# One vector step moved four turns later and one small matmul moved one step later, in a fused decoder kernel on one core

## The chip, the cores and the metric

The kernel runs on one core of one Trainium2 chip. The metric is device time in microseconds (us) of one execution; lower is better. A core has a matrix engine (PE, with its own queue PEld for loading the stationary operand), a vector engine (DVE), an activation engine (ACT), a general engine (POOL) and a queue engine (SP) that here only issues DMA transfers. Each engine works through its own instruction list in order, and they meet at semaphores.

## The reference, cut to what matters

Two sequences of 512 tokens with 1024 channels pass through a layer of three parts: a state-space mixer followed by a gated feed-forward block ("stage one" below), a product with a fake-quantised context, and a second gated feed-forward block whose weights are formed from two tensors ("stage two").

```
h   = res + mamba2(rmsnorm(x, ln1_w), ...)          # eight blocks of 128 channels per sequence
h2  = rmsnorm(h, ln2_w)                             # needs the sum of squares over all channels
mlp = silu(h2 @ gate_w.T) * (h2 @ up_w.T) @ down_w.T        # INTER = 3584
...
q1, q2 = fake_quant(x), fake_quant(ctx);  x = x + q1 @ q2
...
d = w - base                                        # w1/mean_w1, w3/mean_w3, w2/mean_w2
W = base + mean(abs(d)) * sign(d)
x = x + (silu(x @ W1.T) * (x @ W3.T)) @ W2.T
```

## The kernel before, in words

Every fp32 product is made of three fp32r products: each operand is split into a rounded high part (ACT copies it, `hi`) and the rest (DVE subtracts, `lo`), and PE does hi by hi, lo by hi and hi by lo. A **step** of PE is 12 matmuls of 128x128 by 128x512: four blocks of the contraction times these three.

Both feed-forward stages (m = 0 and m = 1) have the same plan. `feed_forward(first, last)` on PE walks numbered steps w. The gate and up weights come in 14 pairs of 256 rows. Pair 0 takes 16 plain steps (`plain`, L1011, steps 0 to 15, counted from the start of the stage); each later pair takes 14 steps of a seven-product scheme (`product`, L1067), so pair 1 has steps 16 to 29 and pair 2 begins with step 30. The down projection follows (`down_step`, L1092). Split weights stand in a ring of seven slots: step w reads slot w % 7, which ACT fills (`ring_hi`, L1323) and DVE completes (`ring_lo`, L1779). PE's step w waits for `ring_lo` of w.

On ACT and DVE, `feed_forward(m)` is a loop over turns i that runs ahead of PE. In turn i DVE makes, where tables say so, a combination of the activations or its low parts (`make`, `part_lo_of`), takes the result of step i - 1 out of PSUM (`gate_up_out`), forms a sum of weights for step i + 6 (`weight_sum`), writes `ring_lo` of step i + 5 (`weight_lo`), and then does one extra job that a table gives to the turn. In stage one the extra job is `coeff_diff` (L1923), a difference of two weight tiles that ACT turns into signs and a sum of absolute values (L1449, L1452). In stage two it is `form_weight` (L1947): one instruction on 128x1024 elements,

```
STT(form_tile(f), sign_in[f % 4], coef[:, kind:kind + 1], form_tile(f), ALU.mult, ALU.add).then_inc(s_form, 1)
```

which turns the raw tile (`raw_odd` for odd pairs, `raw_even` for even ones) into the weights of stage two in place. It waits for the raw tile and for the signs, both brought by SP's DMAs. `FORM_AT` gives the turn of every forming, numbered f. Numbers 0 to 3 are pair 0 and are done before the loop; 4 to 7 are the four tiles of pair 1. Four sign tiles exist, and SP loads the signs of f + 4 one turn after the forming of f. Before the loop begins SP issues the two `raw_odd` loads and the signs of 4 to 7; the first of them waits until all four activation quarters of stage two are made, because they are read from where `raw_odd` is written.

ACT's turn is similar: high parts of activations, `weight_hi` of step i + 5, in stage one the signs and absolute values of the turn before, then copies and SiLU of PE's results. The last SiLU of a pair (L1401) must be done before PE starts the next pair, since both use one PSUM bank.

In front of stage one the mixer's output projection gives sixteen blocks of 128 channels, eight per half (one half is one sequence). DVE adds their squares up (`rms_add`, L2223), and PE sums over partitions with one matmul against ones, `rms_sums(h)` (L983; the trace shows it as two passes). ACT and DVE make the scale of the half from it and then the quarters b12 and b22 of the activations. Quarters b11 and b21 belong to the first half and are made earlier; steps 0 to 7 use only these, so that PE has work while the second half is normalised.

Of the kernel before, what the change touches and what calls it, by code (L numbers as in the profile page):

```python
# [61 lines left out]
BASE_G = (0, NG + ND)  # L62
# [5 lines left out]
def turn_no(p, turn):  # L68
    return turn if p == 0 else NP + 14 * (p - 1) + turn
# [19 lines left out]
def step_of(w):  # L89

    m = 0 if w < W_END[0] else 1
    if w < BASE_G[m] + NP:
        return m, "f", 0, (w - BASE_G[m]) // 2, (w - BASE_G[m]) % 2
    if w < BASE_D[m]:
        p, i = divmod(w - BASE_G[m] - NP, 14)
        return m, "g", p + 1, i // 2, i % 2
    d, k = divmod(w - BASE_D[m], SC_PAIRS)
    return m, "d", d // 7, d % 7, k
# [37 lines left out]
def _form(p, turn, what):  # L136
    FORM_AT[turn_no(p, turn)] = len(FORM_NO)
    FORM_NO[what] = len(FORM_NO)
# [3 lines left out]
for _p in range(PAIRS):  # L142
    if _p == PAIRS - 1:
        for _t in (0, 3, 6, 9):
            _form(_p, _t, ("d", next(_down)))
        continue
    _first = _p == 0
    _form(_p, 3 if _first else 0, ("g", _p + 1, 0, 0))
    if not _first:
        _form(_p, 2, ("d", next(_down)))  # L150
    _form(_p, 5 if _first else 4, ("g", _p + 1, 0, 1))
    _form(_p, 7 if _first else 6, ("g", _p + 1, 1, 0))
    _form(_p, 9 if _first else 8, ("g", _p + 1, 1, 1))
    if not _first:
        _form(_p, 10, ("d", next(_down)))
assert next(_down, None) is None
# [31 lines left out]
def build(nc, x_t, ctx, w_mamba, w_dt, w_gu, w_dn, f_gu, f_dn, b_gu, b_dn, params, shapes_only,  # L188
# [637 lines left out]
    def _(pe):  # L826
# [154 lines left out]
        def rms_sums(h):  # L981
            pe.wait_ge(s_sqd, (KT - 1) * (h + 1))
            pe.matmul(bank(6 + h), ones[:, :], rms_sum[:, h, :], start=True, stop=True).then_inc(s_rv, 1)  # L983
# [15 lines left out]
        def plain(w, m, j, x):  # L999

            pe.wait_ge(s_wlo, w + 1)
            name, quad = PLAIN[j][1:]
            out = bank(PLAIN_BANK[quad][x])
            slot = w % RING
            for kk in range(KH):
                if j in (0, 1, 4, 5) and x == 0:
                    pe.wait_ge(s_tlo, n_lo(m, name, kk))
                col = slice(kk * P, (kk + 1) * P)
                hi, lo = part_hi(m, name)[:, kk, :], part_lo(m, name)[:, kk, :]
                for n, (wt, a) in enumerate(((WRH, hi), (WRH, lo), (WRL, hi))):  # L1010
                    ins = pe.matmul(out, wt[:, slot, col], a, start=j % 2 == 0 and kk == 0 and n == 0,  # L1011
                                    stop=j % 2 == 1 and kk == KH - 1 and n == 2, skip_group_check=True)
            ins.then_inc(s_pd, 1)
# [57 lines left out]
        def down_step(w, m, sc, t, k):  # L1071

            pe.wait_ge(s_wlo, w + 1)
            u = w - BASE_D[m]
            pe.wait_ge(s_ulo, m * ND + u + 1)
            d = sc * 7 + t
            if k == 0:
                if d >= 2:
                    pe.wait_ge(s_do, 4 * (m * 14 + d - 1))
                elif d == 0:  # L1080
                    pe.wait_ge(s_c12, 2 * (PAIRS - 1) * (m + 1))
                else:
                    pe.wait_ge(s_gs, 4 * PAIRS * (m + 1))
                    pe.wait_ge(s_pr[2], PAIRS * (m + 1))
                    if m == 0:
                        pe.wait_ge(s_ab, CF_BLOCKS)
            slot, us = w % RING, u % RING
            for q in range(KH):
                out = bank(4 * (d % 2) + q)
                col = slice(q * P, (q + 1) * P)  # L1090
                for n, (wt, a) in enumerate(((WRH, ur_hi(us)), (WRH, ur_lo(us)), (WRL, ur_hi(us)))):
                    ins = pe.matmul(out, wt[:, slot, col], a, start=t in (0, 1, 3) and k == 0 and n == 0,  # L1092
                                    stop=k == SC_PAIRS - 1 and n == 2, skip_group_check=True)
            ins.then_inc(s_pd, 1)

        def feed_forward(first, last):
            for w in range(first, last):
                m, stage, i, j, l = step_of(w)
                if stage == "f":
                    plain(w, m, j, l)  # L1100
                elif stage == "g":
                    product(w, m, i, j, l)
                else:
                    down_step(w, m, i, j, l)
# [43 lines left out]
                ins = pe.matmul(out, row_weights, mean_rows(b, part).bitcast(F32), start=part == 0, stop=part == 1)  # L1148
            ins.then_inc(s_csumd, 1)

        feed_forward(BASE_G[0], BASE_G[0] + 1)
        rms_sums(1)
        feed_forward(BASE_G[0] + 1, BASE_G[0] + 2)
        pe.wait_ge(s_h, BATCH * KT)
        feed_forward(BASE_G[0] + 2, W_END[0] - 4)
        pe.wait_ge(s_xs, 1)
# [81 lines left out]
    def _(act):  # L1238
# [86 lines left out]
        def inner_hi(w):  # L1325

            m, _, sc, t, k = step_of(w)
            u = w - BASE_D[m]
            gen = 64 * (2 * m + sc + 1)
# [73 lines left out]
        def plain_gate(w):  # L1403

            m, _, _, j, x = step_of(w)
            if j % 2 == 0 or x == 1:
                return
            if j == 1:
                if m == 0:
                    act.wait_ge(s_xsum, 16 * BATCH * KT)  # L1410
                else:
                    act.wait_ge(s_x2, 32 * KT)
                act.wait_ge(s_tv, B22_MADE[m])
            quad = PLAIN[j][2]
            act.wait_ge(s_pd, w + 1)
            act.activation(G[m][:, quad, :], bank(PLAIN_BANK[quad][0]), ACT.Silu).then_inc(s_gs, 1)

        def psum_copy(w):

            m, _, p, t, x = step_of(w)  # L1420
            pp = m * PAIRS + p
            done = 2 * n_before(pp)
            if t == 0:
                if p > 1 and x == 0:
                    act.wait_ge(s_c22, done - 2 + 1)
                elif p > 1:
                    act.wait_ge(s_pr[3], pp)
                act.wait_ge(s_pd, w + 1)
                act.activation(TX[m][:, x, :], bank(BANK_B[x]), ACT.Copy).then_inc(s_x1, 1)
            elif t == 2:  # L1430
                if p > 1 and x == 0:
                    act.wait_ge(s_c12, done - 2 + 1)
                elif p > 1:
                    act.wait_ge(s_pr[1], pp)
                act.wait_ge(s_pd, w + 1)
                act.activation(TU[m][:, x, :], bank(BANK_B[x]), ACT.Copy).then_inc(s_u2, 1)
            elif t == 3:
                if x == 0:
                    act.wait_ge(s_c11, done + 1)
                else:  # L1440
                    act.wait_ge(s_pr[0], pp + 1)
                act.wait_ge(s_pd, w + 1)
                act.activation(TX[m][:, x, :], bank(BANK_C[x]), ACT.Copy).then_inc(s_c5, 1)
# [994 lines left out]
```

## Time and profile before

| quantity | value |
|---|---|
| median of 3 runs | 2155.32 us (2153.18 to 2155.93) |
| the profiled execution, its own time | 2155.74 us |
| its span, first to last instruction | 2153.9 us |
| PE busy | 2105.2 us (98% of the span) |
| DVE busy | 1664.3 us (77%) |
| ACT busy | 1070.0 us (50%) |
| mean granted clock of PE | 0.991 of full speed |

Busy shares are means over the whole program. PE's 98% says that nearly all time is matmuls; what is left to gain or lose is in the few places where PE stands still, and in the matmuls behind a pause that run at a lower clock. A start time printed for a matmul is the one to reckon with: in an undisturbed stream a matmul is shown as 0.39 us long, but the next starts 0.23 us after it.

### The profile page before, as it was taken

The numbers are of one execution on the slowest core, as the hardware profiler recorded it, in microseconds if no ns is written. First come the engines' busy times: TensorE is split into PE (matmuls) and PEld (weight loads), VectorE is DVE, ScalarE is ACT, GpSimd is POOL, SyncE is SP. The second block draws the span as 40 slices with busy tenths as digits, with TensorE's granted clock in tenths as the row PEclk, the third lists the DMA queues.
The fourth block names the chain that finished last, engine by engine and source line by source line (L and its number), as shares of the span: only waits on it lengthen the run. The fifth ranks groups of instructions, "written<-read, shape, count | busy, mean of one in ns | idle before, by whom it ended". The sixth has DMA issues, their size and how long they took to land.

```text
span 2153.9 us, 26614 instructions
## 1 busy us (share of the span) xinstructions
PE 2105.2 (98%) x9266; PEld 1684.2 (78%) x9270; DVE 1664.3 (77%) x2497; ACT 1070.0 (50%) x1764; POOL 182.1 (8%) x296
## 2 busy tenths in 40 slices
PE   7999999999999999999999999899999999999999
PEld 3777778778888878888888854788888888888887
DVE  7776666698777878887979898887777677788885
ACT  4333344457777777774444466443333333444442
POOL 0000110101111111210000002001000000100000
PEclk9999999999999999999999999999999999999999
DMA  3151115638989999888250044554444444756101
GB/s 123 40 186 50 57 59 175 171 75 287 311 294 309 344 320 328 307 308 337 90 184 1 1 166 105 152 186 152 159 171 147 164 147 147 287 194 197 63 20 59
DMA packets 136434, 370.06 MB, mean 172 GB/s; under 512 B 16688, under 2 KB 27568, under 8 KB 132656
## 3 DMA queue, kind: packets, MB, share of 16 engines
q1 hardware_dynamic: 111216, 288.16, 39.1%
q0 software_dynamic: 25088, 80.23, 11.0%
q8 instruction: 73, 1.20, 0.2%
q14 instruction: 57, 0.47, 0.1%
HBM read 288.12 MB, written 84.41 MB: 173 GB/s over the span
## 4 chain that ended last, share of the span: by engine, by line
PE 82%; DVE 10%; ACT 4%; issue 2%; DMA 2%; SPq 0%; DVEq 0%; ACTq 0%
PE pair L1067 41%; PE pair L1092 24%; PE pair L839 6%; PE pair L832 2%; PE pair L1011 2%; DVE conv_out L2099 1%; DMA ctx_in<-ctx 1%; DVE ring_lo L1779 1%; PE pair L949 1%; DVE pair L1923 1%; PE pair L970 1%; PE pair L848 1%; DVE weights_lo L1689 1%; PE pair L1125 1%; PE pair L972 0%
## 5 line engine op out<-in xcount | busy, mean ns | idle before, releaser
L1067 PE MATMUL pair<-comb_hi,ring_hi 128*128 128x512 f32 x1456 | 567.3, 390 | 3.3 <-ACT gate_a L1401 3.3
L1067 PE MATMUL pair<-comb_hi,ring_lo 128*128 128x512 f32 x1456 | 567.2, 390 | 0.0
L1067 PE MATMUL pair<-comb_lo,ring_hi 128*128 128x512 f32 x1456 | 567.1, 389 | 0.0
L1092 PE MATMUL pair<-inner_ring_a,ring_hi 128*128 128x512 f32 x1120 | 344.8, 389 | 0.0
L1067 PEld LDWEIGHTS pair<-comb_hi,ring_hi 128*128 128x128 f32 x1456 | 273.7, 188 | 61.7 <-DVE ring_lo L1779 4.9
L1067 PEld LDWEIGHTS pair<-comb_hi,ring_lo 128*128 128x128 f32 x1456 | 273.7, 188 | 57.0
L1067 PEld LDWEIGHTS pair<-comb_lo,ring_hi 128*128 128x128 f32 x1456 | 273.7, 188 | 56.6
L1092 PEld LDWEIGHTS pair<-inner_ring_a,ring_hi 128*128 128x128 f32 x1120 | 210.2, 188 | 43.5
L1092 PE MATMUL pair<-inner_ring_a,ring_lo 128*128 128x512 f32 x560 | 217.9, 389 | 0.0
L1323 ACT ACTIVATE ring_hi<-ring_sum 128x512 fp32r<-128x512 f32 x160 | 101.0, 632 | 142.0 <-DVE ring_sum L1764 140.3
L1092 PE MATMUL pair<-inner_ring_b,ring_hi 128*128 128x512 f32 x448 | 138.3, 390 | 0.0
L1779 DVE TENSOR_TENSOR ring_lo<-raw_a,ring_hi 128x512 fp32r<-128x512 f32 x146 | 99.4, 685 | 50.1 <-ACT ring_hi L1323 50.1
L1449 ACT ACTIVATE sign_out<-pair 128x1024 int8<-128x1024 f32 x84 | 85.9, 1023 | 80.7 <-DVE pair L1923 80.7
L1092 PEld LDWEIGHTS pair<-inner_ring_a,ring_lo 128*128 128x128 f32 x560 | 105.1, 188 | 21.9
L839 PE MATMUL pair<-act_hi,weights_hi 128*128 128x512 f32 x256 | 109.3, 427 | 1.6 <-DVE act_lo L2168 1.4
L1779 DVE TENSOR_TENSOR ring_lo<-ring_sum,ring_hi 128x512 fp32r<-128x512 f32 x160 | 109.5, 684 | 1.5 <-ACT ring_hi L1323 0.2
L1923 DVE TENSOR_TENSOR pair<-coeff_in 128x1024 f32<-128x1024 f32 x84 | 103.0, 1226 | 0.8 <-DMA coeff_in<-b_gu 0.8
L1689 DVE TENSOR_TENSOR weights_lo<-weights_raw,weights_hi 128x1024 fp32r<-128x1024 f32 x44 | 54.6, 1240 | 59.5 <-ACT weights_hi L1246 31.1
L839 PE MATMUL pair<-act_hi,weights_lo 128*128 128x512 f32 x256 | 100.3, 392 | 0.0
L839 PE MATMUL pair<-act_lo,weights_hi 128*128 128x512 f32 x256 | 100.1, 391 | 0.0
L1092 PEld LDWEIGHTS pair<-inner_ring_b,ring_hi 128*128 128x128 f32 x448 | 84.1, 188 | 17.8 <-issue 0.5
L1323 ACT ACTIVATE ring_hi<-raw_a 128x512 fp32r<-128x512 f32 x146 | 90.3, 625 | 8.4 <-PE pair L1011 5.6
(374 smaller groups left out, 3586.1 us busy)
## 6 DMA issues: line engine op xcount, KB each, us to landing
coeff_in<-f_gu SPq DMA_DIRECT2D x56, 512.0 KB, 5.2
coeff_in<-b_gu SPq DMA_DIRECT2D x56, 512.0 KB, 6.8
weights_raw<-w_mamba SPq DMA_DIRECT2D x44, 512.0 KB, 3.4
raw_a<-w_gu SPq DMA_DIRECT2D x28, 512.0 KB, 7.3
raw_a<-w_gu SPq DMA_DIRECT2D x56, 256.0 KB, 6.3
u_spill<-gate_a POOLq DMA_DIRECT2D x56, 256.0 KB, 5.8
coeff_in<-f_dn SPq DMA_DIRECT2D x28, 512.0 KB, 4.4
coeff_in<-b_dn SPq DMA_DIRECT2D x28, 512.0 KB, 6.6
```

Of the source, the lines that this page charges most:

```text
L832: ins = pe.matmul(out[:, HALF[half]], w[:, wi, k * P:(k + 1) * P], a(half, k), start=k == 0 and n == 0, stop=k == KT - 1 and n == 2)
L839: ins = pe.matmul(out, w[:, wi, k * P:(k + 1) * P], a(b, k), start=k == 0 and n == 0, stop=k == KT - 1 and n == 2, skip_group_check=True)
L848: return pe.matmul(out[:, HALF[b]], ones[:, :], src[:, HALF[b]], start=first, stop=last)
L949: pe.matmul(ps[2][:, g * 512:(g + 1) * 512], bx_cur[:, 2 + g, :], xbc[:, 4 + g * HPG:4 + (g + 1) * HPG, b * SEQ + c * P:b * SEQ + (c + 1) ...
L1011: ins = pe.matmul(out, wt[:, slot, col], a, start=j % 2 == 0 and kk == 0 and n == 0, stop=j % 2 == 1 and kk == KH - 1 and n == 2, skip_gro ...
L1067: ins = pe.matmul(out, wt[:, slot, col], a, start=t in (0, 1, 3) and kk == 0 and n == 0, stop=kk == KH - 1 and n == 2, skip_group_check=True)
L1092: ins = pe.matmul(out, wt[:, slot, col], a, start=t in (0, 1, 3) and k == 0 and n == 0, stop=k == SC_PAIRS - 1 and n == 2, skip_group_chec ...
L1323: act.activation(WRH[:, slot, :], src, ACT.Copy).then_inc(s_whi, 1)
L1449: act.activation(sign_out[:, c % 2, :], dif_ps[:, :], ACT.Sign).then_inc(s_sign, 1)
L1689: TT(WL[:, slot, :], raw[:, rslot, :], WH[:, slot, :].bitcast(F32), ALU.subtract).then_inc(s_ready, 1)
L1779: TT(WRL[:, slot, :], src, WRH[:, slot, :].bitcast(F32), ALU.subtract).then_inc(s_wlo, 1)
L1923: TT(dif_ps[:, :], dif[:, c % 2, 0, :], dif[:, c % 2, 1, :], ALU.subtract).then_inc(s_cd, 1)
```

## The change

Two things are moved, nothing is added or removed. In stage two the four formings of pair 1 stand at turns 7, 8, 9 and 10 in place of 3, 5, 7 and 9. The table serves SP too, so its loads of the signs 8 to 11 move along. On PE the matmul `rms_sums` of the second half stands behind step 1 of stage one in place of behind step 0.

```diff
     _first = _p == 0
-    _form(_p, 3 if _first else 0, ("g", _p + 1, 0, 0))
+    _form(_p, 7 if _first else 0, ("g", _p + 1, 0, 0))
     if not _first:
         _form(_p, 2, ("d", next(_down)))
...
-    _form(_p, 9 if _first else 8, ("g", _p + 1, 1, 1))
+    _form(_p, 10 if _first else 8, ("g", _p + 1, 1, 1))
...
-        feed_forward(BASE_G[0], BASE_G[0] + 1)
+        feed_forward(BASE_G[0], BASE_G[0] + 2)
         rms_sums(1)
-        feed_forward(BASE_G[0] + 1, BASE_G[0] + 2)
         pe.wait_ge(s_h, BATCH * KT)
         feed_forward(BASE_G[0] + 2, W_END[0] - 4)
```

DVE's list in stage two before, from `ring_lo` of step 8 to `ring_lo` of step 12 (`comb_...` are combinations of activations, `gate_b` is a result taken out, `raw_odd<-sign_in...` a forming):

```order
L1779 TENSOR_TENSOR ring_lo<-raw_even,ring_hi 128x512
L1947 SCALAR_TENSOR_TENSOR raw_odd<-sign_in_ab,coeff,raw_odd 128x1024
L1862 TENSOR_TENSOR gate_b<-pair,gate_b 128x512
L1779 TENSOR_TENSOR ring_lo<-raw_even,ring_hi 128x512
L1831 TENSOR_TENSOR comb_lo_f_14_128<-comb_lo_f_15_129,comb_lo_f_14_128 128x512 x4
L1779 TENSOR_TENSOR ring_lo<-raw_even,ring_hi 128x512
L1947 SCALAR_TENSOR_TENSOR raw_odd<-sign_in_ab,coeff,raw_odd 128x1024
L1851 TENSOR_TENSOR comb_lo_115<-comb_lo_f_15_129,comb_hi_85 128x512 x4
L1779 TENSOR_TENSOR ring_lo<-raw_even,ring_hi 128x512
L1834 TENSOR_TENSOR comb_hi_f_16_102<-comb_lo_f_14_128,comb_hi_f_16_102 128x512 x4
L1779 TENSOR_TENSOR ring_lo<-raw_even,ring_hi 128x512
```

The same stretch now, on to the first forming (the line numbers are one lower, since the file has one line less):

```order
L1778 TENSOR_TENSOR ring_lo<-raw_even,ring_hi 128x512
L1861 TENSOR_TENSOR gate_b<-pair,gate_b 128x512
L1778 TENSOR_TENSOR ring_lo<-raw_even,ring_hi 128x512
L1830 TENSOR_TENSOR comb_lo_f_14_128<-comb_lo_f_15_129,comb_lo_f_14_128 128x512 x4
L1778 TENSOR_TENSOR ring_lo<-raw_even,ring_hi 128x512
L1850 TENSOR_TENSOR comb_lo_115<-comb_lo_f_15_129,comb_hi_85 128x512 x4
L1778 TENSOR_TENSOR ring_lo<-raw_even,ring_hi 128x512
L1833 TENSOR_TENSOR comb_hi_f_16_102<-comb_lo_f_14_128,comb_hi_f_16_102 128x512 x4
L1778 TENSOR_TENSOR ring_lo<-raw_even,ring_hi 128x512
L1946 SCALAR_TENSOR_TENSOR raw_odd<-sign_in_ab,coeff,raw_odd 128x1024
```

The first forming stood between `ring_lo` of steps 8 and 9; it now stands behind `ring_lo` of step 12, and the other three behind those of 13, 14 and 15. All four were ahead of `ring_lo` of step 15 before; now three are.

PE's list around `rms_sums` before, at the end of step 0 (`comb_hi_75`, `comb_lo_103` are the first half's activations):

```order
L1011 MATMUL pair<-comb_lo_103,ring_hi 128x512
L1011 MATMUL pair<-comb_hi_75,ring_lo 128x512
L983 MATMUL pair<-rms_sum,ones 128x512
L1011 MATMUL pair<-comb_hi_75,ring_hi 128x512
L1011 MATMUL pair<-comb_lo_103,ring_hi 128x512
```

In the changed list twelve more matmuls of step 1 stand ahead of the L983 row, and behind it the first one of step 2:

```order
L1011 MATMUL pair<-comb_lo_103,ring_hi 128x512
L1011 MATMUL pair<-comb_hi_75,ring_lo 128x512
L983 MATMUL pair<-rms_sum,ones 128x512
L1011 MATMUL pair<-comb_hi_76,ring_hi 128x512
L1011 MATMUL pair<-comb_lo_104,ring_hi 128x512
```

SP's list changes in one place: the signs of 8 to 11 were loaded ahead of both loads of pair 2's raw tile (`raw_even`). The load of the signs of 11 now stands between these two, and its wait for the fourth forming holds back the second of them.


## Rows read from the trace of the kernel before

**Rows 1.** The page: the span.

```profile
span 2153.9 us, 26614 instructions
```

**Rows 2.** Waits of PE, whole span: total us, times, longest us.

```profile
PE pair L1011 <- DVE ring_lo L1779: 7.0, 2, 6.4
...
PE pair L1067 <- ACT gate_a L1401: 3.3, 4, 1.9
...
PE pair L983 <- DVE rms_sum L2223: 2.6, 1, 2.6
```

**Rows 3.** PE in time, stage one: start, length, line, tiles, [idle before <-releaser].

```profile
440.62 0.39 PE L1011 MATMUL pair<-comb_hi,ring_lo 128*128 128x512 f32 x1
443.59 1.12 PE L983 MATMUL pair<-rms_sum,ones 128*128 128x512 f32 x2 [2.57 <-DVE rms_sum L2223]
...
448.20 0.39 PE L1011 MATMUL pair<-comb_hi,ring_hi 128*128 128x512 f32 x1
```

**Rows 4.** PE in time, the same sum of the first half.

```profile
402.88 0.40 PE L839 MATMUL pair<-act_hi,weights_lo 128*128 128x512 f32 x1
...
404.21 0.40 PE L839 MATMUL pair<-act_lo,weights_hi 128*128 128x512 f32 x1
```

**Rows 5.** DVE in time, stage one.

```profile
479.21 1.29 DVE L1779 TENSOR_TENSOR ring_lo<-raw_a,ring_hi 128x512 fp32r<-128x512 f32 x2
...
511.74 0.69 DVE L1881 TENSOR_TENSOR gate_a<-first_copy_a,pair 128x512 f32<-128x512 f32 x1 [2.44 <-PE pair L1067]
512.34 0.68 DVE L1779 TENSOR_TENSOR ring_lo<-raw_a,ring_hi 128x512 fp32r<-128x512 f32 x1
...
514.43 0.69 DVE L1881 TENSOR_TENSOR first_copy_a<-first_copy_a,pair 128x512 f32<-128x512 f32 x1 [0.26 <-PE pair L1067]
...
517.17 0.69 DVE L1891 TENSOR_TENSOR gate_a<-second_copy_a,pair 128x512 f32<-128x512 f32 x1
```

**Rows 6.** ACT in time, stage one.

```profile
511.28 0.63 ACT L1323 ACTIVATE ring_hi<-raw_a 128x512 fp32r<-128x512 f32 x1
...
522.85 0.60 ACT L1401 ACTIVATE gate_a<-pair 128x512 f32<-128x512 f32 x1
```

**Rows 7.** PE in time, first matmul of the third pair of stage one.

```profile
525.04 0.39 PE L1067 MATMUL pair<-comb_hi,ring_hi 128*128 128x512 f32 x1
```

**Rows 8.** PE in time, stage two.

```profile
1357.32 0.39 PE L1011 MATMUL pair<-comb_hi,ring_lo 128*128 128x512 f32 x1
1364.14 0.80 PE L1011 MATMUL pair<-comb_hi,ring_hi 128*128 128x512 f32 x1 [6.43 <-DVE ring_lo L1779]
...
1383.98 0.50 PE L1011 MATMUL pair<-comb_hi,ring_hi 128*128 128x512 f32 x1 [0.60 <-DVE ring_lo L1779]
...
1386.63 0.39 PE L1011 MATMUL pair<-comb_hi,ring_lo 128*128 128x512 f32 x1
```

**Rows 9.** DVE in time, stage two.

```profile
1351.95 0.68 DVE L1779 TENSOR_TENSOR ring_lo<-raw_even,ring_hi 128x512 fp32r<-128x512 f32 x1
1361.60 1.28 DVE L1947 SCALAR_TENSOR_TENSOR raw_odd<-sign_in_ab,coeff,raw_odd 128x1024 f32<-128x1024 int8 x1 [8.97 <-DMA sign_in_ab<-sign_spill]
...
1383.25 0.68 DVE L1779 TENSOR_TENSOR ring_lo<-raw_even,ring_hi 128x512 fp32r<-128x512 f32 x1
```

**Rows 10.** Chain of waits, stage two: start, length, what.

```profile
1350.81 10.69 DMA sign_in_ab<-sign_spill
```

**Rows 11.** ACT in time, stage two.

```profile
1422.90 0.58 ACT L1401 ACTIVATE gate_b<-pair 128x512 f32<-128x512 f32 x1
```

**Rows 12.** PE in time after two other pauses.

```profile
396.86 0.50 PE L839 MATMUL pair<-act_hi,weights_hi 128*128 128x512 f32 x1 [1.42 <-DVE act_lo L2168]
...
795.25 0.47 PE L1067 MATMUL pair<-comb_hi,ring_hi 128*128 128x512 f32 x1 [1.94 <-ACT gate_a L1401]
```

**Rows 13.** Two stretches: us, PE busy (instructions), granted clock, DMA share, GB/s.

```profile
795.20:799.60 4.40, 4.35 (x13) 0.63 0.88 292
1364.10:1369.40 5.30, 5.26 (x12) 0.50 0.19 69
```

More of the change, by code:

```diff
@@ L147 @@
     _first = _p == 0
-    _form(_p, 3 if _first else 0, ("g", _p + 1, 0, 0))
+    _form(_p, 7 if _first else 0, ("g", _p + 1, 0, 0))
     if not _first:
         _form(_p, 2, ("d", next(_down)))
-    _form(_p, 5 if _first else 4, ("g", _p + 1, 0, 1))
-    _form(_p, 7 if _first else 6, ("g", _p + 1, 1, 0))
-    _form(_p, 9 if _first else 8, ("g", _p + 1, 1, 1))
+    _form(_p, 8 if _first else 4, ("g", _p + 1, 0, 1))
+    _form(_p, 9 if _first else 6, ("g", _p + 1, 1, 0))
+    _form(_p, 10 if _first else 8, ("g", _p + 1, 1, 1))
     if not _first:
```

## The prediction, made before the result was known

> **What bounds the kernel now.** I read the page first: the whole program is 2153.9 us long [rows 1] and PE is busy nearly throughout, so time can only be won or lost where PE stands still or runs slowly. The waits of PE say where: `ring_lo` holds it up twice for 7.0 us in all, 6.4 of them at once, the second half's `rms_sum` once for 2.6 us, and the SiLU L1401 four times for 3.3 us [rows 2]. The first two are what the change touches. Then I went to the engines in order of time around both.
>
> An undisturbed PE starts a matmul every 0.2267 us: from the tenth matmul of step 1 at 448.20 [rows 3] to the first of step 30 at 525.04 [rows 7] there are 3 + 28 x 12 = 339 starts in 76.84 us. A step is 2.72 us.
>
> **Stage two.** After `ring_lo` of step 8 (started at 1351.95, done at 1352.63) DVE stands for 8.97 us before the first forming, which waits for its signs [rows 9]. The chain of waits shows these signs issued at 1350.81 and landed 10.69 us later, at 1361.50 [rows 10]. `ring_lo` of step 9 is queued behind the forming, so PE, through with step 8, stands for 6.43 us until 1364.14 [rows 8]. What follows runs at half clock: 0.50 granted from 1364.10 to 1369.40, the 1.2 GHz level [rows 13]. At step 15 it waits again, 0.60 us [rows 8]. Sum: from the last matmul of step 8 (1357.32) to the last of step 15 (1386.63) PE took 29.31 us for 7 x 12 = 84 starts, which undisturbed are 19.04 us. So 10.27 us are to be had.
>
> Can DVE now deliver? An instruction of 0.68 us is followed 0.60 us after its start (511.74 and 512.34 in [rows 5]), so it can go on at 1352.55 instead of 1361.60. From there to the start of `ring_lo` of step 15 at 1383.25 [rows 9] it worked without a pause for 21.65 us; one of the four formings (1.28 long, 1.20 net) no longer stands ahead. 1352.55 + 21.65 - 1.20 = 1373.0, done at 1373.68. Undisturbed, PE reaches step 15 at 1357.55 + 6 x 2.72 = 1373.87. That is 0.2 us to spare, the tightest of these steps. The steps before have more: no forming stands ahead of `ring_lo` 9 to 12, and one more comes with each of 13, 14 and 15.
>
> The forming itself moves to turn 7, behind `ring_lo` of 12. The list shows 17 operations of 512 columns from 1352.55 to there: 17 x 0.60 = 10.2, so it starts at about 1362.8, which is 1.3 us behind the landing at 1361.50 [rows 10]. So its wait is hidden by work that DVE has anyway. All four formings end at about 1373.0 + 0.6 + 1.2 = 1374.8, 1.8 us before PE wants step 16 at 1376.6, and `ring_lo` of 16 is directly behind.
>
> Later on DVE is 9.05 us earlier than before and PE 10.27, so DVE's lead over PE is 1.2 us thinner. Step 16 had 2.3 us (`ring_lo` done at 1383.25 + 0.60 + 0.68 = 1384.53 against 1386.86), and the order of work behind it gives the later ones more. The last place where it counts is the SiLU L1401 before step 30: started at 1422.90, done at 1423.48 [rows 11], now at 1414.43. PE began step 30 at 1386.63 + 0.23 + 14 x 2.72 = 1424.94, now at 1414.67. Again 0.2 us to spare. Value taken: 10.3 us. Bounds: the least is 7, if both margins fail by a microsecond and one pause takes PE's clock down; the most is 10.3, since the stalls hold no more.
>
> SP's loads: the second load of pair 2's raw tile is now held until the fourth forming, about 1 us later against PE than before. DVE needs it only at turn 22, about 19 us after, against some ten for the slowest transfer here [rows 10]. Nothing.
>
> **Stage one.** PE ends step 0, waits 2.57 us for `rms_sum` and starts `rms_sums` at 443.59; behind it the clock is down [rows 3]. From the last matmul of step 0 (440.62) to the tenth of step 1 (448.20) are 7.58 us for ten starts, 2.27 undisturbed. The matmul itself costs, at full clock in the first half, 4.21 - 2.88 = 1.33 us for two starts that would take 0.45: 0.87 us [rows 4]. So the pause with its slow tail costs 7.58 - 2.27 - 0.87 = 4.44 us. With step 1 in front PE arrives at 440.85 + 2.72 = 443.57, when the sum is just ready; `rms_sums` runs at the same moment as before, and nothing on ACT and DVE behind it moves. PE is 4.4 us ahead at step 2.
>
> That lead meets DVE and ACT, which stay where they were. `ring_lo` of step 15 ends at 479.85 [rows 5]; PE now wants it at 444.46 + 13 x 2.72 = 479.82, a tie. In pair 1 DVE and ACT hand each other coefficient differences, signs and absolute values, and only their waits for PE can shrink: 2.44 us before L1881 at 511.74, of which 0.4 count, because the `ring_lo` behind it (512.34) then waits for the `ring_hi` of 511.28 + 0.63 [rows 5, 6]; then 0.26 at 514.43 with some 0.1 of rounding, and 0.2 between there and 517.17, where 2.5 us of work take 2.74 [rows 5]. In all 0.95 us. So L1401, done at 523.45 [rows 6], is done at 522.5. PE wants step 30 at 525.04 - 4.44 + 0.1 = 520.7 and waits some 1.7 us. Of 4.4 us there remain 525.04 - 522.5 - 0.1 = 2.4. From there DVE waits for PE again and keeps in step. Bounds: at least 0.8, if the clock falls behind this new pause (next paragraph); at most 4.4, if L1401 follows PE fully.
>
> Does the clock fall? After a pause of 1.42 us the next matmul was 0.50 long and no slow ones followed; after one of 1.94 us [rows 12] the granted clock was 0.63 over the next 4.4 us: 13 matmuls where 19.4 fit, some 1.5 us lost [rows 13]. The new pause of 1.5 to 1.7 us lies between. I take the milder, as the nearer; the other is a rival. TensorE: Matmul & The Clock Gate, section "What's actually happening", in the Trainium skill, says that the number of slow matmuls at a start differs from run to run of one kernel. No run here shows that yet; by it every slow tail above, those removed too, could be one or two microseconds longer or shorter.
>
> **Sum.** 10.3 + 2.4 = 12.7 us. The profiled execution took 2155.74 us, 1.84 more than its span; less 12.7 that is 2143.0. It stands 0.42 above the median of the runs, so the median should be 2155.32 - 12.7 = 2142.6 us.
>
> **Rivals.**
> - A, the forecast: 2142.6, own range 2141.4 to 2143.8. Chance 0.45.
> - B, stage one keeps all its 4.4 us, because ACT catches up in pair 1. For it: L1401 did not hold PE at this step before [rows 5 to 7]. Against it: the count above. 10.3 + 4.4 = 14.7, so 2140.6. Chance 0.12.
> - C, the new pause before step 30 takes the clock down: 12.7 - 1.5 = 11.2, so 2144.1. Chance 0.18.
> - D, the signs come late. DVE now takes out its result at 1352.55 and POOL stores it (256 KB) while the signs are on their way; before, that store began after 1363. If the signs landed 4 us later, at 1365.5, the first forming would wait 2.75 us and step 15 start 2.55 late, with a slow tail of 1.5: 12.7 - 4.05 = 8.65, so 2146.7. It decides from 1.5 us of lateness on. Chance 0.14. DMA: Bandwidth & Descriptors, section "Issuing engines are not separate DMA queues", in the Trainium skill, says that transfers of SP and POOL run on the same 16 engines and interleave, which speaks for it; the trace shows 10.69 us for one sign tile among them.
> - E, the L1401 region from 690 to 840 us, where it waits already, swallows stage one's gain, as its pace comes from DMA: 10.3, so 2145.0. Chance 0.06.
> - F, the other side: PE, arriving early, pauses before each of the 13 pairs of stage one and each pause costs the slow tail of 1.5 us. 13 x 1.5 = 19.5 against 12.7: slower by 6.8, so 2162.1; it decides from nine pairs on. Against it: a PE that lost 1.5 us is later at the next pair and waits less, and the waits there were four [rows 2]. Chance 0.03.
> - G, the change doesn't do what it says: the first forming finds its raw tile missing, a megabyte issued just before the signs, and stands as long as now. Then only stage one's 2.4 us remain: 2152.9. Against it: at 1361.60 the tile was there. Chance 0.02.
>
> What a measurement can tell from no change is 0.2%, 4.3 us. A to E are faster by more: 0.95; I give 0.94. G is within: 0.03, F slower: 0.03. The range reaches from just under B to just over D: 2140.0 to 2147.0.
>
> **What would show each step.** Right: DVE shows no wait for `sign_in_ab` at the first forming, PE's wait for `ring_lo` is gone or under 0.5 us, and the stretch behind step 8 has full clock; L983 has no wait, and step 2 of stage one starts at about 444.5; PE shows one new wait of 1.5 to 1.7 us for L1401 near 520.7. Wrong: a wait of DVE for signs or for `raw_odd` near 1360 (D, G); half clock behind 522 (C); no wait there (B); L1401 waits in sum over 3.3 + 1.7 us (E, F).

## The result, and the profile after

The changed kernel takes 2142.75 us (median of 5 runs, 2141.25 to 2146.65); the kernel before took 2154.68 us beside it (5 runs, 2153.18 to 2155.93). The ratio is 0.9948, 95% interval 0.9938 to 0.9959, so the change is worth 11.2 us, between 8.8 and 13.4. The forecast was 2142.6. Two executions that took far longer than all others of their kernel (one of the kernel before, 5703.73 us, and one of e4_form5, 2345.16 us) are left out of every median.

The head of the page after, to be held against [rows 1]: PE is busy for 3 us less, though it does the same matmuls (fewer ran at a low clock), and the span is 13.0 us shorter. DVE works as long as before.

```profile
span 2140.9 us, 26618 instructions
...
PE 2101.9 (98%) x9270; PEld 1680.6 (78%) x9270; DVE 1664.3 (78%) x2497; ACT 1071.0 (50%) x1764; POOL 182.5 (9%) x296
```

PE's waits from 430 us on (engine, line, waited for: us in total, times, longest), which answer to [rows 2]:

```profile
PE pair L1067 <- ACT gate_a L1400: 3.3, 5, 1.4
PE pair L1119 <- DVE x_mid L2286: 1.8, 1, 1.8
PE pair L1011 <- issue: 0.7, 1, 0.7
PE pair L1169 <- DVE x_mid L1914: 0.7, 1, 0.7
```

Both lines that the change aimed at, `ring_lo` with 7.0 us and `rms_sum` with 2.6 us, are gone. The SiLU (L1401, now L1400) still costs 3.3 us, but in five pauses in place of four, the longest 1.4 in place of 1.9. That the sum is the same is chance, as the parts below show.

**Stage two.** DVE from `ring_lo` of step 9 on (start, duration, what, and in brackets the idle time before it), to be held against [rows 9]:

```profile
1350.10 0.69 DVE L1778 TENSOR_TENSOR ring_lo<-raw_even,ring_hi 128x512 fp32r<-128x512 f32 x1
...
1359.12 0.70 DVE L1778 TENSOR_TENSOR ring_lo<-raw_even,ring_hi 128x512 fp32r<-128x512 f32 x1
1359.73 1.29 DVE L1946 SCALAR_TENSOR_TENSOR raw_odd<-sign_in_ab,coeff,raw_odd 128x1024 f32<-128x1024 int8 x1
...
1369.93 0.70 DVE L1778 TENSOR_TENSOR ring_lo<-raw_even,ring_hi 128x512 fp32r<-128x512 f32 x1
1370.53 1.30 DVE L1946 SCALAR_TENSOR_TENSOR raw_odd<-sign_in_cd,coeff,raw_odd 128x1024 f32<-128x1024 int8 x1
```

The first forming at 1359.73 has no bracket: it finds its signs, which landed at 1359.25, 0.5 us earlier. `ring_lo` of step 15 starts at 1369.93 and ends at 1370.63; PE begins step 15 some 0.2 us later, at 1370.85 (a step of 2.72 us before step 16, at 1373.57). From the stage's first matmul to the first of step 16 it took 1386.86 - 1331.33 = 55.53 us before, and 1373.57 - 1328.26 = 45.31 us now: 10.22 us less.

**Stage one.** PE at the end of step 1, with the `rms_sums` that caused 2.57 us of waiting and a slow tail in [rows 3]:

```profile
444.06 0.39 PE L1011 MATMUL pair<-comb_hi,ring_lo 128*128 128x512 f32 x1
444.29 1.13 PE L983 MATMUL pair<-rms_sum,ones 128*128 128x512 f32 x2
444.85 0.79 PE L1011 MATMUL pair<-comb_hi,ring_hi 128*128 128x512 f32 x1
445.49 0.40 PE L1011 MATMUL pair<-comb_lo,ring_hi 128*128 128x512 f32 x1
```

It runs at 444.29 without a wait, and step 2's second matmul follows at 445.49 at full speed. Then PE meets the SiLU before step 30, where it waited for nothing before [rows 7]:

```profile
521.60 0.39 PE L1067 MATMUL pair<-comb_hi,ring_lo 128*128 128x512 f32 x1
523.35 0.47 PE L1067 MATMUL pair<-comb_hi,ring_hi 128*128 128x512 f32 x1 [1.36 <-ACT gate_a L1400]
523.65 0.40 PE L1067 MATMUL pair<-comb_lo,ring_hi 128*128 128x512 f32 x1
```

ACT just ahead of it, to be held against [rows 6]:

```profile
522.00 0.20 ACT L1451 ACTIVATION_READ_ACCUMULATOR pair<-pair 128x1 f32 x1
...
522.62 0.59 ACT L1400 ACTIVATE gate_a<-pair 128x512 f32<-128x512 f32 x1
```

L1400 ends at 523.21, and PE, which finished step 29 1.4 us before, starts step 30 at 523.35. Measured from the first matmul of the stage (438.03 before, 438.73 now), step 30 begins after 84.62 us in place of 87.01: 2.39 us earlier.

The chain of waits over both stages (start, length, what) shows the same from its side:

```profile
475.80 7.89 PE pair L1011 x34
483.69 38.31 PE pair L1067 x168
523.35 171.66 PE pair L1067 x756
...
1328.33 45.41 PE pair L1011 x192
1373.74 1.36 PE pair L1067 x6
```

In stage one it leaves PE ahead of 523.35; in stage two it is PE without a break from 1328.33 to the end of step 15, 45.41 us, where [rows 10] had it leave for a DMA of 10.69 us.

**Two things that the change did not aim at.** The pause before 795.25 us, 1.94 us with a slow tail [rows 12, 13], is short now:

```profile
792.25 0.47 PE L1067 MATMUL pair<-comb_hi,ring_hi 128*128 128x512 f32 x1 [0.59 <-ACT gate_a L1400]
```

That gives 2.9 us. And behind PE's wait of 0.7 us for `x_mid` (L1169, at 1257.31; stage two begins at 1328.26) the clock is down now. The two stretches of 6.3 us from the end of this wait on, before and after (columns: stretch, busy time of PE, PEld, DVE, ACT, POOL with counts, granted clock, DMA share, GB/s):

```profile
1261.92:1268.22 6.30, 6.25 (x18) 2.56 (x19) 6.14 (x12) 3.96 (x7) 0.00 (x0) 1.00 1.01 405
```

```profile
1257.31:1263.61 6.30, 6.30 (x12) 2.57 (x13) 6.14 (x12) 3.95 (x7) 0.00 (x0) 0.73 1.00 399
```

The clock of 0.73 takes back 1.55 us. So the gain between the starts of the two stages is 2.39 + 2.93 - 1.55 = 3.77 us. To it come 10.22 in stage two; 0.70 go off because this execution reached stage one later, and 0.24 in a hiccup at 1395 us. Sum: 13.05 us, which is the difference of the last matmuls (2148.23 and 2135.18).

### The profile page after: what moved, and what is told of

It is laid out like the page before. It is cut to its first block, busy times and chain, and to the rows that moved or that the text cites. A ratio compares the mean times of both kernels' runs of the same rounds, so it can differ in the third digit from the quotient of the medians.

```text
span 2140.9 us, 26618 instructions
## 1 busy us (share of the span) xinstructions
PE 2101.9 (98%) x9270; PEld 1680.6 (78%) x9270; DVE 1664.3 (78%) x2497; ACT 1071.0 (50%) x1764; POOL 182.5 (9%) x296
## 4 chain that ended last, share of the span: by engine, by line
PE 87%; DVE 7%; ACT 3%; issue 2%; DMA 1%; SPq 0%; DVEq 0%; ACTq 0%
PE pair L1067 42%; PE pair L1092 24%; PE pair L839 7%; PE pair L1011 4%; PE pair L832 2%; DVE conv_out L2098 1%; PE pair L1125 1%; PE pair L949 1%; PE pair L970 1%; DVE pair L1922 1%; DVE weights_lo L1688 1%; PE pair L848 1%; PE pair L1119 1%; PE pair L972 1%; PE pair L865 0%
## 5 line engine op out<-in xcount | busy, mean ns | idle before, releaser
L1322 ACT ACTIVATE ring_hi<-raw_a 128x512 fp32r<-128x512 f32 x146 | 90.4, 626 | 10.7 <-DVE raw_a L1758 7.1
```

The source lines that it names most:

```text
L1322: act.activation(WRH[:, slot, :], src, ACT.Copy).then_inc(s_whi, 1)
```

## The experiments

Eight kernels ran in two sets of four, each set on one chip with the kernel before beside it. Beside the first four the kernel before took 2155.25 us (15 runs), beside the others 2154.49 us (20 runs). All times are medians; the first four experiments are ctl_after, e1_form, e2_rms and e3_coeff. Where kernels of the two sets are compared, the ratios are the fairer measure. One table for all, worked out from PE's start times; "gate" is the granted clock over the 6.3 us behind PE's wait for `x_mid`:

| kernel | us | ratio (95%) | one: step 0 to 16 | step 0 to stage two | two: step 0 to 16 | gate |
|---|---|---|---|---|---|---|
| before | 2155.25 / 2154.49 | 1 | 48.93 | 893.30 | 55.53 | 1.00 |
| after | 2142.75 | 0.9948 (0.9938-0.9959) | 44.80 | 889.53 | 45.31 | 0.73 |
| ctl_after | 2142.72 | 0.9947 (0.9933-0.9960) | 44.79 | 889.65 | 45.29 | 0.73 |
| e1_form | 2145.07 | 0.9952 (0.9938-0.9965) | 48.94 | 890.03 | 45.28 | 1.00 |
| e2_rms | 2153.08 | 0.9988 (0.9979-0.9997) | 44.82 | 892.50 | 55.74 | 0.73 |
| e3_coeff | 2141.36 | 0.9937 (0.9923-0.9950) | 44.84 | 889.00 | 45.27 | 0.73 |
| e4_form5 | 2149.21 | 0.9976 (0.9966-0.9986) | 44.79 | 888.98 | 51.89 | 0.73 |
| e5_signs | 2150.07 | 0.9979 (0.9969-0.9988) | 48.97 | 890.22 | 51.98 | 1.00 |
| e6_rms2 | 2145.20 | 0.9959 (0.9943-0.9974) | 47.41 | 890.48 | 45.28 | 0.73 |
| e7_best | 2140.33 | 0.9935 (0.9922-0.9949) | 44.80 | 886.99 | 45.29 | 0.73 |

The two columns "0 to 16" repeat to 0.05 us wherever the code is the same, with one exception: stage two takes 55.53 us in the kernel before and 55.74 in e2_rms. "Step 0 to stage two" does not repeat: it holds pauses and slow tails that come and go from one execution to the next.

### The change again: ctl_after

> The changed kernel again, beside its parts. Both theories: 12 to 13 us faster than before, no wait of DVE for signs in stage two, a PE wait of about 1.4 us for the SiLU L1400 before step 30. What differs from its first profile is what varies from run to run. Theory 1 (the two stalls alone explain the gain, 10.2 + 2.4 us; the pause of 1.94 us at 795 us and its slow tail in the first profile of before, gone in that of after, were chance): a pause of over 1 us or a slow tail somewhere in 690 to 840 us may come back here. Theory 2 (the lead of PE changes how the context's transfers meet the loop, and so takes that pause away for good): none of the four waits between 690 and 840 us is over 0.7 us.

Measured: 2142.72 us, and both columns as in the first profile. The pause for L1400 at 790.92 is 0.65 us long and has no slow tail, as in the first profile of this kernel.

### Each half alone: e1_form and e2_rms

e1_form keeps the new turns of the formings and has `rms_sums` back behind step 0; e2_rms is the other way about.

```diff
# e1_form, against after
-        feed_forward(BASE_G[0], BASE_G[0] + 2)
+        feed_forward(BASE_G[0], BASE_G[0] + 1)
         rms_sums(1)
+        feed_forward(BASE_G[0] + 1, BASE_G[0] + 2)
# e2_rms, against after: turns 3, 5, 7, 9 in place of 7, 8, 9, 10
```

> Only the formings moved to turns 7 to 10; the sum of squares stays behind step 0. Theory 1: 10.2 us faster than before (10.0 to 10.5), PE waits 2.6 us at L983 as before and not at all for ring_lo in stage two. Theory 2: the same 10.2 us, and the long pause near 795 us is there as in before. Rival that the second move is what lets DVE keep up in stage two: would leave a wait for ring_lo there, 8 us or less.

> Only the sum of squares moved behind step 1; the formings stay at turns 3, 5, 7, 9. Theory 1: 2.4 us faster; L983 without a wait, a PE wait of 1.4 us for L1401 before step 30 that before has not, the 6.4 us wait for ring_lo in stage two unchanged. Theory 2: 4 to 5.3 us faster, since the pause at 795 us and its slow tail go too.

Measured: 2145.07 and 2153.08 us, so 10.2 and 2.2 us under the kernel before; their sum, 12.4, is what both together gave (12.5). PE's waits in e1_form:

```profile
PE pair L983 <- DVE rms_sum L2223: 2.6, 1, 2.6
PE pair L1119 <- DVE x_mid L2287: 1.8, 1, 1.8
PE pair L1067 <- ACT gate_a L1401: 1.8, 4, 0.4
```

and in e2_rms:

```profile
PE pair L1011 <- DVE ring_lo L1778: 7.7, 2, 7.4
PE pair L1067 <- ACT gate_a L1400: 4.8, 5, 2.1
```

Each has the stall that its undone half is there to remove, and not the other. The table says the same: 45.28 against 55.53 for the formings, 44.82 against 48.93 for the sum. In e2_rms the stall for `ring_lo` is even longer, 7.7 us. That is not the lead from stage one, which does not count within stage two: in this execution the stage began at full clock (1.00 over its first 6.3 us, against 0.73 in the kernel before), so PE came earlier to signs that landed as late as before.

The two also settle the pause near 795 us. The second theory had PE's lead from stage one remove it for good. But e2_rms, which has the lead, has the pause, 2.12 us long and with its slow tail, 0.62 granted over 4.4 us:

```profile
795.37 0.76 PE L1067 MATMUL pair<-comb_hi,ring_hi 128*128 128x512 f32 x1 [2.12 <-ACT gate_a L1400]
```

```profile
795.37:799.80 4.43, 4.43 (x13) 3.54 (x14) 2.86 (x5) 3.09 (x5) 1.08 (x2) 0.62 0.83 291
```

e1_form, which has no lead, has a pause of 0.43 us at 795.18 instead. So the lead is neither needed for the pause to go nor enough to remove it; what decides it is not shown. The 2.9 us found there in the first pair of profiles can't be put down to the change.

### The signs' margin: e4_form5

```diff
-    _form(_p, 7 if _first else 0, ("g", _p + 1, 0, 0))
+    _form(_p, 5 if _first else 0, ("g", _p + 1, 0, 0))
```

> The changed kernel with only the first of the four formings earlier, at turn 5 (behind ring_lo of step 10) in place of turn 7; the others stay at 8, 9 and 10. It asks how near the cliff the change stands. Theory 1 (the signs' landing, about 11 us after their issue, is what the first forming waits for): with the stage starting at about 1327 DVE reaches this forming at about 1353.5, the signs land at about 1358, so DVE stands some 4.5 us, ring_lo of step 11 is late and PE stalls some 3 us, with a slow tail behind it of 1 to 2 us: 4 to 5 us over the changed kernel, about 2147. Rival: the landing follows the wish, or DVE's work in front was what mattered, so that two turns earlier cost nothing: within 1 us of the changed kernel, no wait of PE for ring_lo. Beside it: a clock of 0.73 in the 6.3 us behind PE's wait for x_mid near 1256 was seen in all four profiled kernels with the sum of squares behind step 1, and full clock in both that have it behind step 0. If the place of the sum decides that, this kernel shows 0.73; if it is luck, either.

Measured: 2149.21 us, 6.5 us over the changed kernel (6.0 by the ratios, whose intervals lie apart). DVE around the first forming:

```profile
1350.91 0.69 DVE L1778 TENSOR_TENSOR ring_lo<-raw_even,ring_hi 128x512 fp32r<-128x512 f32 x1
1357.34 1.28 DVE L1946 SCALAR_TENSOR_TENSOR raw_odd<-sign_in_ab,coeff,raw_odd 128x1024 f32<-128x1024 int8 x1 [5.74 <-DMA sign_in_ab<-sign_spill]
1358.54 0.69 DVE L1850 TENSOR_TENSOR comb_lo<-comb_lo_f,comb_hi 128x512 fp32r<-128x512 f32 x1
```

PE in front of the step that waits, and the clock behind it:

```profile
1359.37 0.76 PE L1011 MATMUL pair<-comb_hi,ring_hi 128*128 128x512 f32 x1 [4.21 <-DVE comb_lo L1850]
```

```profile
1359.37:1364.10 4.73, 4.73 (x11) 3.75 (x12) 4.73 (x9) 0.00 (x0) 0.00 (x0) 0.51 0.12 31
```

The first theory holds: DVE waits 5.74 us for the signs. Two sizes were off. PE waits not 3 but 4.21 us, and not for `ring_lo` but for the low part of a combination (L1850), which is queued behind the forming and is wanted for step 10; and the clock of 0.51 behind it costs 2.4 more, so the stage loses 51.89 - 45.29 = 6.6 us. The signs landed at 1357.23, which is 31.2 us after the stage's first matmul. In the changed kernel the first forming starts 31.5 us after it. By this execution the margin is 0.3 us, not the 1.3 of the prediction. In the six profiles with the first forming at turn 7 it is 0.3 to 1.0 us. Turn 6 was not tried; it would stand five operations of 0.60 us, 3.0 us, earlier, and so by this estimate turn 7 is the earliest that is free.

### What the first forming waits for: e5_signs

```diff
# against before
         spill_x2(0)
+        for f in range(4, 8):
+            load_sign(f)
         spill_x2(1)
         load_second(1, 0)
         load_second(1, 1)
-        for f in range(4, 8):
-            load_sign(f)
```

> The kernel before, with its formings at turns 3, 5, 7 and 9 and its sum of squares behind step 0, but SP issues the four sign tiles of stage two's second pair ahead of the second spill of x2, some 10 us earlier in the stream of transfers, and the raw tiles of pair 1 stay where they were. Two things are needed by the first forming: the signs and the raw_odd tile. Theory 1 (the signs are only the last to land of a queue that is short as a whole: the raw tile is issued at about 1349, a microsecond or two ahead of the signs, and a tile of this queue takes 9 to 12 us): DVE's wait before the first forming shrinks by less than 2 us, from 9.0 to 7 or more, and the time is 2153 to 2155. Rival (only the signs are late, the raw tile lands in 3 to 4 us): the wait goes from 9.0 to under 2 us, PE's stall of 6.4 us goes, and the time is 2146 to 2149. Beside it: full clock behind PE's wait for x_mid near 1262 if the place of the sum of squares decides that, 0.73 or 1.00 if it is luck.

Measured: 2150.07 us, by the ratio 4.5 us (2.6 to 6.7) under the kernel before. DVE:

```profile
1353.08 0.68 DVE L1779 TENSOR_TENSOR ring_lo<-raw_even,ring_hi 128x512 fp32r<-128x512 f32 x1
1358.96 1.29 DVE L1947 SCALAR_TENSOR_TENSOR raw_odd<-sign_in_ab,coeff,raw_odd 128x1024 f32<-128x1024 int8 x1 [5.20 <-DMA raw_odd<-b_gu]
```

PE, twice held up, and the clock behind each of the two pauses:

```profile
1361.51 0.50 PE L1011 MATMUL pair<-comb_hi,ring_hi 128*128 128x512 f32 x1 [2.70 <-DVE ring_lo L1779]
...
1366.40 0.47 PE L1011 MATMUL pair<-comb_hi,ring_hi 128*128 128x512 f32 x1 [1.89 <-DVE comb_lo L1851]
```

```profile
1361.50:1364.20 2.70, 2.69 (x12) 2.17 (x12) 2.70 (x5) 2.12 (x4) 0.22 (x1) 1.00 0.38 137
1366.40:1370.80 4.40, 4.39 (x12) 3.50 (x13) 4.40 (x8) 0.00 (x0) 0.00 (x0) 0.61 0.11 34
```

Neither theory holds; the truth lies between. The wait shrank from 8.97 to 5.20 us, and its releaser is now the raw tile. That tile landed 26.5 us after the stage's first matmul, the signs before at 30.2 us. So the raw tile hides behind the signs, 3.7 us ahead of them, and earlier signs alone could never give more than that: the stage gained 55.53 - 51.98 = 3.55 us. The changed kernel's formings stand behind both landings.

### One step later still: e6_rms2

```diff
-        feed_forward(BASE_G[0], BASE_G[0] + 2)
+        feed_forward(BASE_G[0], BASE_G[0] + 3)
         rms_sums(1)
```

> The changed kernel with the sum of squares one step later still, behind step 2 instead of step 1. Theory 1 (behind step 1 PE arrives just when the sum is ready, and what hangs on it, the chain over ACT and DVE, is then as early as it can be; a step more delays this chain by 2.7 us): ring_lo of the steps 7 and 8 comes 1.5 to 2 us late for PE, so a wait of PE for ring_lo or for a combination near 457, 1 to 3 us slower than the changed kernel, 2144 to 2146. Rival (there is slack behind the sum, the place behind step 1 is one of several): no new wait before 480, the wait for L1400 near 522 of the same 1.4 us or longer by up to 1, the time within 1 us of the changed kernel. Beside it: a clock of 0.73 behind PE's wait for x_mid near 1256 if the place of the sum decides it.

Measured: 2145.20 us, 2.5 us over the changed kernel by the medians (the two ran in different sets, and the intervals of their ratios overlap). DVE in front of the late step, and PE at it:

```profile
448.20 0.69 DVE L2227 SCALAR_TENSOR_TENSOR rms_steps<-rms_scale 128x512 f32<-128x512 f32 x1 [5.22 <-ACT rms_scale L1574]
...
458.41 0.69 DVE L1778 TENSOR_TENSOR ring_lo<-raw_a,ring_hi 128x512 fp32r<-128x512 f32 x1
```

```profile
459.15 0.50 PE L1011 MATMUL pair<-comb_hi,ring_hi 128*128 128x512 f32 x1 [1.48 <-DVE ring_lo L1778]
```

DVE now stands 5.22 us, until 448.20, for what hangs on the sum (2.61 us in the changed kernel). `ring_lo` of the step at 459.15 is late by 1.48 us, and with four hiccups of 0.2 to 0.3 us behind it PE reaches step 16 2.6 us later (47.41 against 44.80). By these rows the first theory holds. The wait before step 30 stays:

```profile
524.68 0.47 PE L1067 MATMUL pair<-comb_hi,ring_hi 128*128 128x512 f32 x1 [1.34 <-ACT gate_a L1400]
```

It comes 87.21 us after the stage's start, 2.6 later than in the changed kernel, since ACT's chain is later by one step as well. Up to step 30 the gain of stage one is lost. At PE's wait for `x_mid` this kernel is still 2.7 us behind the changed one, but at the start of stage two only 0.9, because one slow tail on the way (L1119, below) was 1.7 us shorter in this execution; so the profiled execution shows less of the loss than the medians. Of the three places tried, only the one behind step 1 serves both PE and the chain.

### The pause before step 30: e3_coeff, and a better version: e7_best

```diff
# e3_coeff, against after
-CF_TURNS = {p: (1, 3, 5, 7, 9, 11, 13) if p <= 9 else ...
+CF_TURNS = {p: (3, 5, 7, 9, 11, 13) if p == 1 else (1, 3, 5, 7, 9, 11, 13) if p <= 10 else ...
# e7_best, against e3_coeff: pair 7 has (1, 3, 6, 8, 11, 13), pair 11 seven turns,
# and the formings stand at 7, 8, 10, 11
```

> The changed kernel with one coefficient difference fewer in pair 1 of stage one (turns 3, 5, ... 13 in place of 1, 3, ... 13) and one more in pair 10. Theory 1 (the lead of 4.4 us is cut to 2.4 before step 30 because DVE and ACT are tied to each other by the coefficient job): one round of that job is 5.1 us, so the wait for L1400 before step 30 goes, step 30 starts 2.0 us earlier against step 0, and the kernel is 1.5 to 2 us faster than the changed one; up to 0.5 of it may return as a short pause in pair 10. Rival (the wait there comes from something else, the stored result of the pair before or the down-going clock): the wait stays at 1 to 1.4 us and the time that of the changed kernel.

> The version with the coefficient blocks moved (pair 1 has six turns in place of seven, pair 10 seven) and two edits more. First: pair 7, which also carries two context tiles, has six coefficient turns, and pair 11 seven, because PE waits for L1400 0.4 to 1.0 us behind each of the pairs 6 to 10 there. Second: the formings stand at turns 7, 8, 10 and 11, so that only two of them, not three, stand ahead of ring_lo of step 15, at which PE waited 0.45 us in that version. Theory 1 (DVE's and ACT's load in the pairs 6 to 10 sets these five waits, and one block less is worth about 2 us of it): the waits for L1400 sum to 1.0 to 2.2 us in place of 3.0, none for ring_lo of step 15, the time 1 to 2.5 us under the one before it, 2139 to 2141 by the median of the runs. Rival (each of these waits is set by the order within its own turn, not by a load that adds up): the waits behind the pairs 8 to 10 stay at 0.4 to 0.6 each, only pair 7's goes, and pair 11 gets one of its own: no gain over 0.5 us.

e3_coeff: 2141.36 us, 1.4 under ctl_after, where its first theory had 1.5 to 2, and their intervals overlap. Step 30 starts 1.7 us earlier than in ctl_after (82.92 us after step 0 against 84.60), but between the starts of the two stages only 0.65 us are left of it. PE's waits, and the one at which the gain is met again:

```profile
PE pair L1067 <- ACT gate_a L1400: 3.0, 5, 1.0
...
PE pair L1011 <- DVE ring_lo L1778: 0.4, 1, 0.4
```

```profile
712.45 0.47 PE L1067 MATMUL pair<-comb_hi,ring_hi 128*128 128x512 f32 x1 [0.99 <-ACT gate_a L1400]
```

The pause of 1.36 us before step 30 is gone, so the coefficient job of pair 1, which loads both DVE and ACT, was its cause. Pair 6's pause grew from 0.54 to 0.99, and pair 10, which has the block now, got one of 0.42 at 867.85. In stage two this execution shows how thin the margin at step 15 is. The stage began without slow matmuls (granted clock 1.00 over its first 6.3 us, 0.73 in the changed kernel, where they cost 1.6 us). PE met DVE instead: near 1335 it lost 0.8 us in small delays, one of them a wait of 0.24 us for a low part (L1850), and at step 15 it came 0.8 us earlier than in the changed kernel and had to wait:

```profile
1368.66 0.68 DVE L1778 TENSOR_TENSOR ring_lo<-raw_even,ring_hi 128x512 fp32r<-128x512 f32 x1
```

```profile
1369.39 0.50 PE L1011 MATMUL pair<-comb_hi,ring_hi 128*128 128x512 f32 x1 [0.45 <-DVE ring_lo L1778]
```

The sum up to step 16 is 45.27 us all the same. Where the stage starts with as many slow matmuls as in the changed kernel, PE alone sets that time; where it starts at full clock, DVE does, and what the clock gives is lost in waits for DVE.

e7_best: 2140.33 us, the fastest of all, ratio 0.9935 (0.9922 to 0.9949). By the medians it is 14.2 us under the kernel before and 2.4 under the changed one; only the first is beyond the intervals. Against e3_coeff, which ran in the other set, the ratios differ by 0.0002, well within their intervals. The waits for L1400:

```profile
PE pair L1067 <- ACT gate_a L1400: 2.7, 5, 1.0
```

2.7 us in place of 3.0: pair 7's pause went, but pair 8's grew to 0.99, and pair 11 got one of 0.44. This is the rival's case, nearly: a block taken out of one pair frees PE there, and the next pairs take it up. No wait for `ring_lo` of step 15 is seen. But this execution had the slow start (0.73 over the first 6.3 us, 45.29 us to step 16), with which the changed kernel doesn't wait either, so whether the new turns help is not shown.

## Why the prediction was right, step by step

**The stall of stage two, 10.3 us: right.** 10.22 in the first profile, 10.24 to 10.26 in ctl_after, e1_form and e3_coeff. The method, counting starts at 0.2267 us against the time taken, gave the size to 0.1 us, tail included.

**DVE ready for step 15 with 0.2 us to spare: right, and the reason for the size.** `ring_lo` ended at 1370.63, 0.2 us before PE wanted it. The prediction did not say that this margin rests on the slow matmuls with which the stage began in its trace; e3_coeff, without them, had to wait.

**The first forming 1.3 us behind the signs' landing: right in kind, the size off.** No wait in any of the six kernels with turn 7. But e4_form5 puts the margin at 0.3 us. The start of the forming was forecast exactly (31.47 us after the stage's first matmul, as measured), but the landing was taken from [rows 10] as if it stayed put. It came 30.2 us after the stage's start in the trace of before, 31.0 in that of the changed kernel and 31.2 in e4_form5. The rival D (signs late) was nearer than its chance said: by its own count it decides from 1.5 us of lateness on, and up to 1.0 us of that was there.

**The rival G (raw tile missing): wrong, and e5_signs says by how much.** The raw tile is 3.7 us ahead of the signs.

**Stage one, stall and tail 4.44 us: 4.1.** PE reaches step 16 48.93 - 44.80 = 4.13 us earlier. The term was 0.3 too large. Of this, 0.16 are a new hiccup near 481 us, where PE now catches up with DVE, in the tie that the prediction found for step 15. Another 0.1 is `rms_sums` itself: from the matmul ahead of it to the second behind it are 445.49 - 444.06 = 1.43 us, against the 1.33 taken from [rows 4].

**Of it 2.4 us remain at step 30: right.** 2.39 in the first profile, 2.4 in ctl_after and e2_rms as well. The pause was forecast as 1.5 to 1.7 us and is 1.36 in the profile's bracket, 1.60 by the starts (521.60 to 523.35 less one of 0.23 is 1.52, and the next start comes 0.07 late). That the chain of DVE and ACT in pair 1 sets it is shown by e3_coeff, which took a block out of the chain and had no pause.

**No slow tail behind the new pause (against C): right in every kernel that has the pause.** After, ctl_after, e2_rms, e4_form5 and e6_rms2 have 1.34 to 1.37 us there, and each goes on at full clock. The prediction had 0.45 for it against 0.18, from one pause of 1.42 us.

**Not foreseen: what comes behind.** The prediction let 2.4 us stand until the end. In the profiles they were changed twice on the way. The pause near 795 us went in one execution and not in another. And the clock behind the wait for `x_mid` is 0.73 in all seven profiles with the sum behind step 1 or 2, and 1.00 in all three with it behind step 0. The first six profiles suggested this grouping, and the four later ones bore it out; e2_rms and e5_signs:

```profile
1262.00:1268.30 6.30, 6.25 (x11) 2.58 (x13) 6.14 (x12) 3.95 (x7) 0.00 (x0) 0.73 1.01 406
```

```profile
1263.06:1269.36 6.30, 6.24 (x18) 2.57 (x19) 6.15 (x12) 3.96 (x7) 0.00 (x0) 1.00 1.00 398
```

By this stage one's half would be worth 2.4 - 1.5 = 0.9 us at the end, and between the starts of the stages the profiles do show only 0.8 (e2_rms against before) and 0.4 (ctl_after against e1_form). The medians say 2.2 (2155.25 less 2153.08) and 2.35 (e1_form less ctl_after), but with an interval of 0.6 to 4.5. Which it is stays open.

What could link a matmul to a clock 800 us later? Not that PE comes earlier or later as such. Counted from stage one's first matmul, the wait for `x_mid` ends after 817.75 to 819.75 us in five profiles with 0.73, after 820.62 and 820.84 in two with 1.00, after 821.24 and 821.57 in two with 0.73, and after 823.89 in one with 1.00. Nor does the clock fall at a fixed distance behind the wait. In the changed kernel the low clock begins 0.57 us behind its end, in e6_rms2 1.3 us; until then both ran at full clock:

```profile
1257.31:1257.88 0.57, 0.57 (x2) 0.33 (x3) 0.57 (x2) 0.00 (x0) 0.00 (x0) 1.00 0.89 374
```

```profile
1258.71:1260.01 1.30, 1.30 (x3) 0.65 (x4) 1.30 (x3) 0.00 (x0) 0.00 (x0) 1.00 1.02 429
```

So the clock seems to change at moments of its own, and the place of the sum may act only by shifting PE against them; a shift of 0.4 us (820.84 and 821.24) goes with the other outcome. This fits all ten profiles but was not tested: no run shifted PE there and left the sum in its place on purpose.

**Luck in the number.** The forecast time was met to 0.2 us, but the single runs of the changed kernel lie 5.4 us apart. The gain by the ratio is 11.2 us (8.8 to 13.4) against 12.7 forecast, and 12.5 by the medians in the later set. The gain of stage two is confirmed to 0.1 us; what stage one brings at the end is not, and the two effects behind it that nobody forecast, 2.9 us won and 1.55 lost in the first pair of profiles, partly cancel.

**The rule on the clock.** The Trainium skill, TensorE: Matmul & The Clock Gate, section "What's actually happening", says that the number of slow matmuls at the start of a kernel differs from run to run. The prediction carried this over to the slow matmuls behind a pause and had no run for it. The traces here agree: the tail behind the wait for `x_mid` at the end of the mean (L1119, six matmuls) took 4.23 to 4.51 us in seven of ten profiles and 2.81 in three. The times of single runs go with the clock too: of the five runs of the changed kernel the two slowest (2145.74 and 2146.65 us) have a mean granted clock of 0.991, the three fastest (2141.25 to 2142.75 us) 0.993 or 0.994.

## What to carry to other kernels

An instruction that waits for a transfer costs what is queued behind it on its engine, so first ask how late it may stand, not how early the transfer may come; behind the slowest of its inputs there can be another, a few microseconds ahead (here 3.7). A lead won by PE lasts until the next engine that has none, so follow it to that engine's own chain before it is put into a sum. And a margin of 0.2 us between two engines, counted from one trace, held here as long as the clock in that stretch was the same, while one against the landing of a DMA was not good to a microsecond.

## What the runs showed of the hardware

The length of a pause does not by itself decide whether PE's clock falls behind it. In e5_signs a pause of 2.70 us was followed by full clock (1.00 over the next 2.7 us), and one of 1.89 us, five microseconds on, by 0.61 over 4.4 us. Nor does the low clock begin with the end of a pause: behind `x_mid` it began 0.57 us later in one execution and 1.3 us later in another. Seven pauses of 1.17 to 1.48 us cost no tail (five before step 30, one of 1.17 in e4_form5 at 791 us, one of 1.48 in e6_rms2); those of 1.94 and 2.12 us near 795 did; and one of 0.67 us ahead of stage two did in seven profiles and did not in three.

The landing of a transfer moves from execution to execution. The first of the four sign tiles (128 KB) landed 30.2 to 31.2 us after the first matmul of stage two in the nine profiles in which SP issued it at the same place, 10.7 to 12.5 us after its issue.
